# Deformable tiles of a fused image network: the stages' weights in the plan that places them

## What is computed

```
x = x + focal(_gn(x))      # q, ctx, gates = linear(x); three depthwise convolutions 3x3, 5x5, 7x7 with gelu; modulator; layer norm; linear
x = x + linear8(_gn(x))    # layer norm; rows rounded to 8-bit floats; w1 (64 -> 512); relu(a) * b; rounded again; w2 (256 -> 64)
x = x + gated(_gn(x))      # four 7x7 circular convolutions as products of spectra, 8 steps of a gated recurrence, linear
x = x + deform(_gn(x))     # below
```

```
val = gather(y0, x0) * ((1 - wy) * (1 - wx)) + gather(y0, x0 + 1) * ((1 - wy) * wx) + gather(y0 + 1, x0) * (wy * (1 - wx)) + gather(y0 + 1, x0 + 1) * (wy * wx)
out = einsum("bhwkc,kcf->bhwf", val, kernel) + bias
```

## Time and profile before

| | |
|---|---|
| median of 3 runs | 6727.5 us (6727.36 to 6736.02) |
| the profiled execution's own time | 6720.37 us |
| its span in the profile | 6718.6 us |
| mean granted clock of PE, full speed being 1 | 0.595 |
| busy share of PE, DVE, ACT, POOL | 60%, 50%, 26%, 43% |
| gathers of POOL (L2067) | 2592, mean 1104 ns |
| HBM read and written | 621.76 MB and 117.51 MB |

### The profile page before, as it was taken

How to read it: one execution, slowest core, us unless ns; L and a number is a source line. 1 busy time by engine, 2 the same in 40 slices (tenths; PEclk the granted TensorE clock), 3 DMA queues, 4 the chain that set the end, 5 groups by cost and what they waited for, 6 DMA issues and landing times. The chain is left out here.

```text
span 6718.6 us, 66875 instructions
## 1 busy us (share of the span) xinstructions
PE 4037.8 (60%) x26416; PEld 3590.6 (53%) x26416; DVE 3327.1 (50%) x4118; ACT 1743.2 (26%) x3401; POOL 2877.0 (43%) x2617
## 2 busy tenths in 40 slices
PE   5864375678745576579644486667755465365333
PEld 4852275677633575468633385567643365364332
DVE  4357533534578544444478544353468734443332
ACT  2124234311233224321223234321223223022000
POOL 0000002534456544443455543544446645556676
PEclk9955555568555555558555555558655555555555
DMA  2830444458332844448423654439632474843332
GB/s 48 174 53 15 73 115 98 111 131 177 76 84 80 162 130 116 107 107 188 93 77 89 126 134 128 120 88 198 120 91 70 98 161 107 169 128 102 100 94 83
DMA packets 864530, 742.19 MB, mean 110 GB/s; under 512 B 667266, under 2 KB 744482, under 8 KB 860866
## 3 DMA queue, kind: packets, MB, share of 16 engines
q1 hardware_dynamic: 739802, 398.02, 29.9%
q0 software_dynamic: 124416, 339.90, 18.1%
HBM read 621.76 MB, written 117.51 MB: 110 GB/s over the span
## 5 line engine op out<-in xcount | busy, mean ns | idle before, releaser
L2067 POOL DMA_INDIRECT e_gb<-corner_table,e_idx x2592 | 2861.8, 1104 | 3820.5 <-DVE e_vw L2128 1842.4
L2128 DVE TENSOR_TENSOR e_vw<-e_gb,e_pc 128x1024 f32<-128x1024 f32 x576 | 756.4, 1348 | 500.4 <-DMA e_gb<-corner_table,e_idx 260.0
L2081 PE MATMUL e_pw<-wk,e_vt 128*128 128x64 f32 x2304 | 501.6, 391 | 614.8 <-ACT e_vt L2105 284.6
L2081 PEld LDWEIGHTS e_pw<-wk,e_vt 128*128 128x128 f32 x2304 | 471.7, 301 | 667.4 <-ACT e_vt L2105 400.2
L2094 PE MATMUL e_pv<-shifts,e_vw 128*128 128x128 f32 x2304 | 504.0, 392 | 169.4 <-DVE e_vw L2132 109.8
L2094 PEld LDWEIGHTS e_pv<-shifts,e_vw 128*128 128x128 f32 x2304 | 444.8, 222 | 175.1 <-DVE e_vw L2132 112.8
L492 PE MATMUL b_p<-b_x,b_tt 100*100 100x96 f32 x4096 | 423.7, 264 | 42.5 <-issue 42.5
L1467 PE MATMUL d_p<-d_wd,d_px 120*96 120x48 f32 x2048 | 345.4, 355 | 162.1 <-DMA d_px<-x_halo 86.4
L492 PEld LDWEIGHTS b_p<-b_x,b_tt 100*100 100x100 f32 x4096 | 410.4, 181 | 52.8 <-issue 51.7
L1467 PEld LDWEIGHTS d_p<-d_wd,d_px 120*96 120x96 f32 x2048 | 343.3, 258 | 167.7 <-DMA d_px<-x_halo 88.7
L2104 ACT ACTIVATE e_vt<-e_pv 128x512 f32<-128x512 f32 x288 | 171.0, 594 | 872.3 <-PE e_pw L2094 429.5
(11 more groups left out here) (306 smaller groups left out, 7623.5 us busy)
## 6 DMA issues: line engine op xcount, KB each, us to landing
b_tt<-zl SPq DMA_DIRECT2D x256, 234.0 KB
b_tt<-zl SPq DMA_DIRECT2D x128, 390.0 KB
e_gb<-corner_table,e_idx POOLq DMA_INDIRECT x2592
d_px<-x_halo SPq DMA_DIRECT2D x32, 1152.0 KB
corner_table<-f_xn SPq DMA_DIRECT2D x128, 288.0 KB
f_xall<-xpad SPq DMA_DIRECT2D x10, 2400.0 KB
d_wd<-zl SPq DMA_DIRECT2D x10, 1890.0 KB
x_halo<-d_xo SPq DMA_DIRECT2D x128, 144.0 KB
```

Source lines behind the costliest of these rows:

```text
L2067: nc.gpsimd.indirect_dma_start(self.gb[k][:, 4 * q:4 * q + 4, :].rearrange("p a c -> p (a c)"), None, T.table[m], off)\
L2081: nc.tensor.matmul(o, self.vt[:, q, :], T.wk[:, q, :], start=(q == 0), stop=False)
L2128: v.tensor_tensor(dst, self.gb[k][:, 4 * k0:4 * k1, :].rearrange("p (k a) c -> p k a c", a=4), bc(w, [128, k1 - k0, 4, C], 3), ALU.mult).t ...
```

## The change

The weight of every step is multiplied by a factor of its stage before `plan()` uses it: 0.5 in A, B and C, 1.4 in L, 1 in D and F.

```diff
@@ -2158,6 +2158,7 @@
     return parts


+SHARE = (0.5, 0.5, 0.5, 1.4, 1.0, 1.0)
 PARTS = parts_of([(NI,)] * (NGRP - 1) + [(2, 2)])


@@ -2181,7 +2182,7 @@

 def plan():

-    steps = sequence()
+    steps = [(s, P, k, w * SHARE[s]) for s, P, k, w in sequence()]
     clock, starts, n = 0.0, [], 0
     for s, P, k, w in steps:
         clock += w
```

## The result

The change is slower. Its median is 6766.4 us (four runs, 6758.0 to 6789.8), the median of the kernel before over four runs 6727.4 us (6717.4 to 6736.0): a ratio of 1.006, 95% interval 1.004 to 1.008, or +39 us. Timed again beside other kernels on another chip it was 6775.6 against 6732.2 us, 1.0072 (1.0055 to 1.0089).

A forecast was written before the change was run, and what follows sets the result against it. No engine was full; after the change POOL was to bound L. The rounds summed to −16 us, late signals after long gather runs added 110, so +94 us, 6821 us; 8-in-10 range 6670 to 6930 us.

The forecast's parts named there:

- 3 × 4.5 + 4 × 6.3 + 5 × 5.7 = 67 us less per round: A, B and C: 3, 4 and 5 tiles fewer, at 4.5, 6.3 and 5.7 us each; bounds 49 and 71 us.
- term 3: L: POOL needs 14.3 us per tile (14.1 in round four) and bounds the stage: at least +40, +40 and +62 us.
- term 5: L: long runs of gathers make PE's signals late, three, three and four episodes at 11 us, 110 us together.
- far under 94: L of round two: POOL's waiting for DVE to free a buffer, 94 us before, would mostly vanish.
- The sign I had named: L of round two: DVE would wait for e_gb, the gathered data, which it did not do before.
- The condition I had read: L and F: PE's signals come late after some 30 gathers without a pause; runs of 27 showed nothing.
- One tile in D: 4 us: D of rounds two and three: one more tile costs 4 us (0 to 5), weighed where DVE is idle anyway.
- F: 28 us forecast: F: 7 us per added tile, so 14, 7 and 7 us in rounds two to four.
- That DVE alone sets L: Rival: POOL keeps up in L and DVE sets its time; −59 us, 6668 us, chance 0.25.
- the main sum: All rounds: +7, −9, −16 and +2 us, together −16 us, and with the long runs +94 us.
- What the Trainium skill: L: tensor_tensor does not stall DMA, so gathers take near 0.95 us and POOL is no limit; chance 0.03.
- POOL sets L, no signal comes late: Rival: POOL bounds L but PE's signals stay prompt; −16 us, 6711 us, chance 0.17.
- Much slower: Rival: five late-signal episodes in each L at 15 us; +209 us, 6936 us, chance 0.10.

The follow-up runs named there:

- light gathers in L: Only 5 of 9 gathers for tiles weighed in L: in the change 6532.6 us (0.9816), in the kernel before 6629.7 us (0.9959).
- light gathers: From the third tile on only 5 of 9 gathers per tile, everywhere: in the change 5927.3 us (0.8803), in the kernel before 5913.1 us (0.8788).
- one memset: The change with one small POOL memset, waited for, after each gather of tiles weighed in L: 6777.2 us, 1.0077 against the kernel before.
- the five runs with 13 tiles: Runs with 13 tiles in F of round two, among them L's weight alone at 1.4 (0.9952) and F's alone at 0.8 (0.9996); F took 305 to 317 us.

## Why the prediction was right and wrong

- **The sign held, and half of the mechanism.** Slower, and PE's signals late beside dense gathers are what turned a gain into a loss: with light gathers in L the same move gains 97 us. POOL as the bound of L, the other half, did not hold. The time, 6766 us, lies in the range, but the forecast of +94 us was more than twice the +39 us measured. Of the 55 us between them 30 are the scatter of the two profiled executions; 25 are in the stages. That it is only 25 is luck: A to C, F of rounds two to four and the last F were 79 us shorter than their terms, L, D and F of round one 54 us longer.
- **"3 × 4.5 + 4 × 6.3 + 5 × 5.7 = 67 us less per round" failed most.** It measured 89, 85 and 78 us, above even the stated bound of 71: 50 us too little in all. I divided round two's excess over round one by its tiles, a mean; the tiles taken away cost 6.9, 7.4 and 7.7 us each in round two. Over three rounds A gave back 54 us where the term has 41, B 72 where it has 76, C 125 where it has 86: the miss is C's for the most part. In C the late signals that I looked for only in L and F were there before the change: DVE's waits in C of round two of the kernel before (L986 and L997 take PE's results there),

```profile
DVE c_sq L986 <- PE c_p L921: 43.4, 7, 18.6
DVE c_sq L986 <- remote: 22.5, 4, 14.6
DVE c_xo L997 <- PE c_p L929: 13.5, 10, 2.0
DVE c_xo L997 <- remote: 10.5, 2, 9.0
```

and in C of the change:

```profile
DVE c_sq L986 <- PE c_p L921: 39.1, 12, 11.5
DVE c_xo L997 <- PE c_p L929: 14.7, 10, 2.2
...
DVE c_xo L997 <- remote: 1.6, 1, 1.6
```

Of 33 us without a named releaser 1.6 are left. The late hand-overs from PE in C fell from 40, 47 and 54 us to 8, 7 and 8, and with light gathers, where there are hardly any, the same tiles give back only 9, 7 and 10 us in C. B was priced well, and by its clock no more can be said of it. In round two the granted clock rose from 0.85 to 0.89, but in round three, here before and after, it stayed the same while B fell by 26 us:

```profile
2995.00:3207.00 212.00, 187.37 (x1650) 177.38 (x1648) 88.95 (x126) 30.74 (x68) 82.02 (x77) 0.87 0.88 187
```

```profile
2999.00:3185.00 186.00, 168.02 (x1548) 159.66 (x1548) 65.60 (x108) 27.79 (x58) 33.57 (x33) 0.87 0.86 175
```

PE is busy for nine tenths of B, and 19 of the 26 us are PE's busy time.
- **"27 tiles × 14.3 = 386 us" (term 3) was wrong in its working.** 14.3 us took the mean gather, with the 57 us that DVE's work beside the gathers adds, and multiplied it. The added gathers cost 0.94 + 0.30 us, so POOL's time in L is 287 + 71 = 358 us, and POOL was idle for DVE for 87 us still, where I had said "far under 94". The sign I had named, DVE waiting for `e_gb`, came out at 6 us. In the change POOL isn't the bound of L, but it stands close behind: with one memset L gained only 16 us, and DVE's wait for gathers grew from 6 to 24.
- **"Five times in 243, I take three" and "11 us each" (term 5) were 33, 33 and 44 us where 57, 56 and 53 were measured.** In place of the 40, 40 and 62 us of term 3 there were 36, 32 and 41, DVE's share. Together the forecast for L was 73, 73 and 106 us, measured 93, 88 and 94. The condition I had read, 30 gathers in a run, was wrong: the 11 clean runs of 27 had taken 44 to 48 us, not 34, because L's DVE operations had stretched their gathers. In the change a run of 27 that took 35 us ends with the late signal shown above. So the slower pace of the 11 is the likelier reason that they were clean; the memsets speak for it too.
- **"One tile in D: 4 us" measured 11 and 12, and 14 in round four, where the term had nothing.** I said it was weighed where DVE is idle anyway, and that was so, though its gathers had stood behind the patch loads and it waited for them. In D of round two of the change (L1467 are the matmuls on the patches, L1518 the sigmoids on ACT that take their results):

```profile
2282.88 5.50 PE L1467 MATMUL d_p<-d_wd,d_px 120*96 120x48 f32 x32 [10.86 <-DMA d_px<-x_halo]
...
2283.43 1.22 DVE L2128 TENSOR_TENSOR e_vw<-e_gb,e_pc 128x1024 f32<-128x1024 f32 x1 [15.29 <-DMA e_gb<-corner_table,e_idx]
...
2288.73 0.33 ACT L1518 ACTIVATE region<-d_p 96x192 f32<-96x192 f32 x1 [19.97 <-PE d_p L1467]
...
2300.05 0.33 ACT L1518 ACTIVATE region<-d_p 96x192 f32<-96x192 f32 x1 [10.35 <-remote]
```

The weighing was over when ACT released the next step of D, L1595, at 2289.1. What came late is again PE's signal to ACT: the matmuls for the second L1518 end at 2288.38, it starts at 2300.05, behind a run of 27 gathers that ends at 2296.8. Before the change, when POOL paused at that place, it started in the moment they ended:

```profile
2275.38 0.33 ACT L1518 ACTIVATE region<-d_p 96x192 f32<-96x192 f32 x1 [1.13 <-PE d_p L1467]
```

From D's first matmul to this second L1518 it is 38 us before and 49 us after, which is nearly all of D's +11 in round two. In round three the second L1518 waited the same 10.35 us. Round four was not taken apart.
- **F: 28 us forecast for rounds two to four, 8 measured.** The two added tiles of round two cost nothing and two fewer gave back 36 us: where a tile falls between the steps matters as much as how many there are. The late hand-overs from PE in F go the same way: 85, 89 and 29 us before in rounds two to four, 71, 63 and 49 in the change, and 44 to 58 in round two of the five runs with 13 tiles. No run separates them from the tiles' own cost.
- **The rivals.** That DVE alone sets L (6668 us, 0.25) fell with L at 440 us; it is what the kernels with light gathers in L do. Its sum leaves out the 8 us for D that the main sum has; with them it is 6676 us. What the Trainium skill ("SBUF — State Buffer", Who interferes with whom) says of tensor_tensor, counted in it at 0.03, fell with the mean of 1.180 us. "POOL sets L, no signal comes late" (6711 us) fell too. "Much slower" had the number of late signals nearly right, 53 to 57 us per L against 75, but not the gain in A to C.

What stays open is how POOL's gathers keep PE's signals from the other engines: only PE's were seen late among those of PE, ACT and DVE in L, the bytes have nothing to do with it, the pace has. Whether it is the number of descriptors or of instructions was not tried, since one gather takes one index per partition.

## What to carry to other kernels

Before moving work to the stage where it looks cheapest, price what is added at the margin and not at the stage's mean: here a tile in L cost 3.7 us on the average of the first 18 and 10 to 11 us from there on, when the move gave back 7 us elsewhere. Take the price of a queue's added work apart from the disturbance that is there anyway (0.94 us against a mean of 1.30). And when no engine is full, look for hand-overs that come late without a named releaser, in every stage, those that give work away included; work that is thinned out on the disturbing engine shows in one run what they cost.

## What the runs showed of the hardware

- PE's signals to ACT and DVE come late (to DVE by 8.7 us in the rows of L above) while POOL issues indirect gathers every 1.25 us; the two shown at the end of a run arrived 3.9 and 3.3 us after its last gather. At 1.35 us per gather the sum of late hand-overs in L of round two fell from 88 to 47 us, at 1.69 us to 0, as it is where there are no gathers at all.
- A gather of 0.95 us took 2.0 us on average beside a DVE tensor_tensor on two SBUF tiles (L1254, L1255).
- It doesn't depend on the bytes: a quarter of each row left L at 439 us and the whole at 6763 us. With five ninths of the gathers the kernel took 807 us less, 12%.
- A waiting POOL is dear: a pause each three tiles made the kernel before 514 us slower and the change some 380.
- Gathers issued beside the loads of the patches, with the DMA engines full, landed 13 to 16 us after they had left POOL, others some 1.4 us after.
